# Sixteen-head attentions with their side work behind each quad of heads, and a spiking layer whose spikes TensorE counts

## The chip, the cores and the metric

The kernel runs on one core of a Trainium2 chip. The metric is the device time of one execution in microseconds (us). Engines are named as in the profile: PE (TensorE matmul), PEld (TensorE weight load), DVE (VectorE), ACT (ScalarE), POOL (GpSimd), SP (SyncE, which issues the DMAs here).

## The reference, cut to what matters

The whole is a stack of twelve small layers on 2048 tokens of 128 features, all in float32. Three of its stages matter here. The two sixteen-head attentions have heads of 8 features and 256 tokens a batch; the second is a mixture of two experts and stands twice in the stack, the first is causal and stands once:

```python
# L1 attention, 8 batches of 256 tokens, 16 heads of 8
scores = jnp.einsum('bhqd,bhkd->bhqk', q, k) * scale
scores = jnp.where(causal, scores, jnp.finfo(scores.dtype).min)
out = jnp.einsum('bhqk,bhkd->bhqd', jax.nn.softmax(scores, axis=-1), v)
return jnp.einsum('btc,cd->btd', out, w_out) + b_out
# L3 attention: the same without the mask, for M = 2 experts, mixed by mha_probs
scores = jnp.einsum('mbhtk,mbhsk->mbhts', q, kk) / jnp.sqrt(jnp.float32(KD))
ctx = jnp.einsum('mbhts,mbhsk->mbthk', jax.nn.softmax(scores, axis=-1), v)
# spiking layer (twice), y = relu(x W_fc)^2 W_proj, five steps
reset = spike_fn(mem - THRESHOLD)
mem_new = BETA * mem + y - reset * THRESHOLD
spk = spike_fn(mem_new - THRESHOLD)          # the output is the mean of spk over the steps
```

## The kernel before, in words

**Order.** Each engine runs a program written out by hand, stage after stage; a stage starts on an engine when all four compute engines have left the one before. Features lie on the partitions, tokens on the free axis. Within a stage the engines meet by semaphores; a wait stands in program order, so everything behind it on that engine waits too. All matmuls but some transposes go through the helper `mm`, so the trace gives them line 195. In the rows, x16 or x4 after a matmul counts instructions; one f32 matmul is two of them.

**SmallHeads** is the base class of `L1Attend` (8 units, one a batch) and `L3Attend` (16 units, two a batch, one an expert). A unit is 16 heads of one batch. `steps()` counts steps s; k = s // 16 is the unit and i = s % 16 the head of the score that is computed at this step. On TensorE a step holds, in this order: side work at certain i, the score of head i of unit k (two matmuls, bank 0, 1 or 5), at odd s the shifted scores of a pair of heads that lag 25 steps behind (`pair_at`, four matmuls into banks 2 to 4), and at every fourth step the weighing of four heads, called a quad here (`quad_at`: 16 f32 matmul instructions with 128x18 weights, which are the exponentials' partners, the values). Quads stand at i = 2, 6, 10, 14 in L3Attend and at i = 0, 4, 8, 12 in L1Attend.

What the other engines do with them: DVE takes the maxima of each score (L1229, or L1227 with the causal mask). A score of step s waits until the reduction of step s-3 is done. ACT takes the exponential of each head of a pair (L1208). A pair waits until the first exponential of the pair before is done (`exped`, 2g - 1). A quad waits for all exponentials of its four heads; in L1Attend it waits for POOL's causal selection of them (L1251).

The side work goes through PSUM bank 7, one group after the other, in both kernels:
- i=0: projection of q and k of unit k+2 (L1091); ACT adds the biases (L1182), POOL splits them into three bf16 parts (L1272 to L1279), and SP takes them through DRAM into the stacks (L1302, L1316), from which the scores of unit k+2 are computed.
- i=3: the maxima of unit k-1, which POOL split (L1258 to L1264), turned by a matmul with the identity (L1100); ACT copies them (L1190), SP moves them into the stacks (L1294). The first pair of the unit waits for that.
- i=5: the raw weighed sums of unit k-3, which ACT copied (L1214), transposed by four matmuls (L1110); DVE takes the reciprocals (L1235) and scales (L1238, raises `scaled`).
- i=7: the values of unit k (L1118), which wait for `scaled` of unit k-3; ACT copies them (L1373 in L1Attend, L1877 in L3Attend).
- i=9: the scaled context transposed again (L1124); ACT adds the bias (L1377, L1882).
- i=11, at the end of a batch: the output projection (`out_tensor`) and DVE's addition (`out_vector`, L1384, L1892).

**Spike.** After a norm, TensorE computes up and down projections of four chunks of 512 tokens, ACT relu and square and the copy of y (L970), and DVE five steps of the neuron a chunk: the membrane with opposite sign (L979), a comparison into the running count (L981), four times the decay (L983), the reset (L985) and the count (L987), then the addition to the residual (L989).

Of the kernel before, what the change touches and what calls it, by code (L numbers as in the profile page):

```python
# [926 lines left out]
class Spike(Stage):  # L927


    def __init__(self, k):  # L930
        super().__init__(k, "spike")
        a = self.arena
        self.h = a.take(TOKENS)
        self.norm = Norm(k, k.X, self.h, "eps5", a.take(TOKENS), a.take(TOKENS))
        self.relu = [a.take(4 * CHUNK) for _ in range(2)]
        self.y, self.mem, self.u, self.acc = (a.take(TOKENS) for _ in range(4))
        self.up, self.relued, self.squared = (self.sig(n, 4 * NCHUNK) for n in ("up", "relued", "squared"))
        self.down, self.copied = self.sig("down", NCHUNK), self.sig("copied", NCHUNK)

    def tensor(self, eng, ch):  # L940
# [4 lines left out]
        for c in range(NCHUNK):  # L945
            self.norm.wait_done(eng, max(c, 1))
            for j in range(4):
                self.wait_ge(eng, self.relued, 4 * c + j - 3)
                mm(ps[:, j, :], k.wp("L1f", "fcT")[:, j * P:(j + 1) * P], self.h[:, chunk(c)]).then_inc(self.up.sem, 1)
            ob = 4 + c % 2  # L950
# [5 lines left out]
            m.then_inc(self.down.sem, 1)  # L956

# [14 lines left out]
    def vector(self, eng, ch):  # L972
        k, V = self.k, self.k.nc.vector
        self.norm.vector(eng, ch)
        for c in range(NCHUNK):
            cs = chunk(c)
            y, mem, u, acc = self.y[:, cs], self.mem[:, cs], self.u[:, cs], self.acc[:, cs]
# [12 lines left out]


class SmallHeads(Stage):
# [9 lines left out]
    def __init__(self, k, name, group, tag, members, causal):  # L1002
# [23 lines left out]
        self.n1 = P if causal else SEQ  # L1026
        U, H = self.units, HEADS
# [16 lines left out]
    def steps(self):  # L1044

        for s in range(-2 * HEADS, HEADS * (self.units + 2) + 12):
# [29 lines left out]
    def heads_tensor(self, eng):  # L1076
        k_, ps, mm, T, U = self.k, self.k.ps, self.k.mm, self.k.nc.tensor, self.units
        for s, k, i in self.steps():
            if s == 1 - 2 * HEADS:
                self.route_tensor(eng)  # L1080
            u = k + 2
            if i == 0 and self.is_unit(u):
                self.wait_ge(eng, self.biased, u)
                self.wait_ge(eng, self.v_copied, k)
                self.wait_ge(eng, self.ctx_copied, k - 3)
                self.wait_out(eng, k - 4)
# [6 lines left out]
            u = k - 1  # L1093
            if i == 3 and self.is_unit(u):
                self.wait_ge(eng, self.mx_split, u + 1)
                self.wait_ge(eng, self.biased, min(k + 3, U))
                self.wait_ge(eng, self.ctx_copied, k - 3)
                self.wait_out(eng, k - 4)
# [3 lines left out]
            u = k - 3  # L1102
            if i == 5 and self.is_unit(u):
                self.wait_ge(eng, self.raw_copied, u + 1)
                self.wait_ge(eng, self.mx_copied, min(k, U))
                self.wait_ge(eng, self.v_copied, min(k, U))
                self.wait_out(eng, k - 4)
# [4 lines left out]
            if i == 7 and self.is_unit(k):  # L1112
                self.wait_ge(eng, self.biased, min(k + 3, U))
                self.wait_ge(eng, self.mx_copied, k)
                self.wait_ge(eng, self.scaled, k - 2)
                ms, b0 = self.member(k), k // self.members * SEQ
# [3 lines left out]
            if i == 9 and self.is_unit(u):  # L1120
                self.wait_ge(eng, self.scaled, u + 1)
                self.wait_ge(eng, self.v_copied, min(k + 1, U))
                for t in range(2):
                    o = T.transpose(ps[:, 7, t * P:(t + 1) * P], self.ctx[:, t * P:(t + 1) * P], k_.K("ident"))  # L1124
                o.then_inc(self.turned_again.sem, 1)
            if i == 11 and self.ends_batch(u):
                self.wait_ge(eng, self.ctx_copied, u + 1)
                self.out_tensor(u // self.members)
# [43 lines left out]
    def heads_scalar(self, eng):  # L1172
        k_, ps, S = self.k, self.k.ps, self.k.nc.scalar
        for s, k, i in self.steps():
            if s == 1 - 2 * HEADS:
                self.route_scalar(eng)
            u = k + 2
            if i == 0 and self.is_unit(u):
# [5 lines left out]
            u = k - 1  # L1184
            if i == 3 and self.is_unit(u):
# [5 lines left out]
            if i == 7 and self.is_unit(k):  # L1191
                self.wait_ge(eng, self.valued, k + 1)
                self.wait_ge(eng, self.weighed, self.QUADS * (k - 2))
                if k == 0:
                    self.wait_ge(eng, self.cleared, 1)
                    self.wait_prepared(eng)
                self.values_scalar(k).then_inc(self.v_copied.sem, 1)
            u = k - 3
            if i == 9 and self.is_unit(u):
# [16 lines left out]
    def heads_vector(self, eng, ch):  # L1216
        ps, V = self.k.ps, self.k.nc.vector
        for s, k, i in self.steps():
# [12 lines left out]
            u = k - 3  # L1231
            if i == 5 and self.is_unit(u):
# [7 lines left out]
            if i == 11 and self.ends_batch(u):  # L1240
                self.wait_ge(eng, self.summed, u // self.members + 1)
                self.out_vector(u // self.members)
# [103 lines left out]
class L1Attend(SmallHeads):  # L1346
# [28 lines left out]
    def context_scalar(self, eng, u):  # L1375
        self.wait_ge(eng, self.summed, u - 1)
        self.k.nc.scalar.activation(self.ctxT[u % 2], self.k.ps[:, 7, 0:SEQ], ACT.Identity, bias=self.k.C("vL1_0")).then_inc(self.ctx_copied.sem, 1)  # L1377

    def out_tensor(self, b):
        self.k.mm(self.k.ps[:, 7, 0:SEQ], self.k.wp("L1a", "wo"), self.ctxT[b % 2]).then_inc(self.summed.sem, 1)  # L1380
# [878 lines left out]
```

## Time and profile before

The time is the median of three runs. The profile comes from an execution of its own, in which some 1.7 us lie around the span.

| what | value |
|---|---|
| median of 3 runs (2144.8 to 2148.79) | 2145.94 us |
| profiled execution | 2153.13 us |
| its span | 2151.4 us |
| PE busy | 1720.4 us, 80% |
| DVE busy | 1294.6 us, 60% |
| ACT busy | 1156.7 us, 54% |
| POOL busy | 609.8 us, 28% |
| chain that ended last | PE 55%, DVE 17%, ACT 14%, issue 7% |

How to read it: a busy PE is not PE at its peak, since matmuls are pipelined and their ends are modelled; a matmul counts as busy until its last result is written. "Start to start" of two neighbours is therefore the better measure of what a group takes. An idle engine costs nothing unless it is on the chain that sets the end. The stages in question lie at about 999 to 1054 us and 1222 to 1279 us (Spike), 1054 to 1222 us (L1Attend), and, for the two L3Attend, their pairs run from about 1490 to 1710 us and from 1860 to 2083 us.

### The profile page before, as it was taken

Reading aid. Unit: us, or ns where it says so; the run is one execution under the profiler, and the core shown is the slowest. Engines: PE = TensorE matmul, PEld = TensorE weight load, DVE = VectorE, ACT = ScalarE, POOL = GpSimd, SP = SyncE. Lnnn points to the kernel's source line nnn. Section 1 sums busy time; section 2 is a strip of 40 time slices with the busy share of each in tenths; the row PEclk is TensorE's granted clock in tenths of the full one; section 3 lists DMA queues with packets and bytes.
Section 4 is the critical chain, followed back from the end, with each engine's and each line's share of the span. In section 5 each row is a group of like instructions: output and inputs, shape, how many; then the busy total and the mean of one; then the engine's idle time right before and its main releaser. Section 6 shows DMA issues by size and latency. Waiting matters only on the chain.

```text
span 2151.4 us, 36562 instructions
## 1 busy us (share of the span) xinstructions
PE 1720.4 (80%) x13656; PEld 904.2 (42%) x13656; DVE 1294.6 (60%) x2595; ACT 1156.7 (54%) x2714; POOL 609.8 (28%) x759
## 2 busy tenths in 40 slices
PE   5896889788898879879468864986999777799976
PEld 1554345533355425543234322333555352355435
DVE  4773477444676357734667276835878445577844
ACT  3664356434465436554336545562888726388862
POOL 2551055200453025410155202303332020333202
PEclk8998999999899899989768687995999978599997
DMA  4000000000000000000063000005444020544403
GB/s 170 16 17 6 0 16 16 12 0 1 16 12 16 1 11 16 12 6 0 8 117 65 2 0 1 0 0 100 95 95 88 2 78 0 109 96 93 80 2 98
DMA packets 55270, 79.19 MB, mean 37 GB/s; under 512 B 6004, under 2 KB 38996, under 8 KB 54584
## 3 DMA queue, kind: packets, MB, share of 16 engines
q1 hardware_dynamic: 52536, 68.47, 14.5%
q0 software_dynamic: 2560, 8.39, 1.4%
q8 instruction: 111, 1.82, 0.4%
q14 instruction: 63, 0.52, 0.1%
HBM read 50.59 MB, written 16.88 MB: 31 GB/s over the span
## 4 chain that ended last, share of the span: by engine, by line
PE 55%; DVE 17%; ACT 14%; issue 7%; POOL 3%; DMA 3%; SPq 0%; DVEq 0%; POOLq 0%; ACTq 0%
PE ps L195 51%; ACT arena L544 4%; ACT arena L1208 2%; DVE arena L1229 2%; PE ps L463 2%; DVE arena L600 2%; ACT arena L267 2%; ACT arena L269 2%; DVE arena L643 1%; DVE arena L985 1%; DVE arena L987 1%; ACT arena L263 1%; DVE arena L983 1%; DMA arena<-scratch 1%; DVE arena L612 1%
## 5 line engine op out<-in xcount | busy, mean ns | idle before, releaser
L195 PE MATMUL ps<-arena 32*64 32x128 f32 (+10 forms) x10192 | 724.0, 319 | 129.9 <-ACT arena L1208 28.1
L195 PEld LDWEIGHTS ps<-arena 128*18 128x18 f32 (+6 forms) x10192 | 412.3, 128 | 434.8 <-issue 120.7
L1229 DVE TENSOR_REDUCE arena<-ps 128x2 f32<-128x512 f32 x512 | 322.4, 684 | 111.1 <-PE ps L195 109.1
L195 PE MATMUL ps<-arena,w_L0f 128*128 128x512 f32 (+3 forms) x800 | 352.1, 573 | 39.5 <-ACT arena L291 14.5
L1208 ACT ACTIVATE arena<-ps 128x512 f32<-128x512 f32 (+1 forms) x640 | 333.8, 576 | 78.7 <-PE ps L195 69.5
L544 ACT ACTIVATE arena<-ps,arena 128x128 f32<-128x128 f32 x512 | 226.2, 461 | 137.8 <-DVE arena L645 137.8
L195 PEld LDWEIGHTS ps<-arena,w_L0f 128*128 128x128 f32 (+2 forms) x800 | 149.4, 204 | 174.4 <-issue 127.0
L195 PE MATMUL ps<-arena,const 128*128 128x512 f32 (+1 forms) x528 | 173.1, 618 | 60.7 <-DVE arena L1657 22.3
L715 POOL TENSOR_TENSOR arena<-arena 128x512 f32<-128x512 f32 x128 | 132.2, 1040 | 239.6 <-DVE arena L617 239.6
L600 DVE TENSOR_TENSOR arena<-ps,arena 128x1024 f32<-128x1024 f32 x128 | 153.3, 1206 | 21.1 <-PE ps L195 21.1
L555 ACT ACTIVATE arena<-ps 128x512 f32<-128x512 f32 x128 | 76.8, 600 | 126.1 <-DVE arena L600 123.4
L707 POOL TENSOR_TENSOR arena<-arena 128x512 f32<-128x512 f32 x64 | 81.2, 1269 | 218.3 <-DVE arena L600 215.5
L195 PEld LDWEIGHTS ps<-arena,const 128*128 128x128 f32 (+1 forms) x528 | 57.7, 156 | 161.9 <-issue 73.5
L643 DVE TENSOR_REDUCE arena<-ps 128x8 f32<-128x1024 f32 x64 | 78.3, 1223 | 71.8 <-PE ps L195 71.6
L612 DVE COPY arena<-ps 128x512 f32<-128x512 f32 x128 | 88.2, 689 | 48.4 <-PE ps L463 48.4
L463 PE MATMUL ps<-const,arena 128*128 128x128 f32 x512 | 80.2, 280 | 34.8 <-issue 26.5
L544 ACT ACTIVATION_READ_ACCUMULATOR arena<-ps,arena 128x1 f32 x512 | 106.5, 208 | 0.0
L1227 DVE CUSTOM_DVE_ANT_0 arena<-ps,masks_b 128x128 bf16<-128x128 f32 (+1 forms) x256 | 75.0, 353 | 43.6 <-PE ps L195 43.3
L463 PEld LDWEIGHTS ps<-const,arena 128*128 128x128 f32 x512 | 57.4, 142 | 96.3 <-issue 94.4
L195 PE MATMUL ps<-residual,const 128*128 128x512 f32 x96 | 58.4, 718 | 44.0 <-DVEq L2094 31.6
L1258 POOL CAST arena<-arena 128x32 bf16<-128x32 f32 x40 | 8.4, 209 | 286.1 <-DVE arena L1229 280.2
L708 POOL TENSOR_TENSOR arena<-arena 128x512 f32<-128x512 f32 x64 | 83.4, 1303 | 0.0
(223 smaller groups left out, 2150.0 us busy)
## 6 DMA issues: line engine op xcount, KB each, us to landing
scratch<-arena SPq DMA_DIRECT2D x40, 384.0 KB, 2.8
arena<-scratch SPq DMA_DIRECT2D x80, 192.0 KB
arena<-scratch SPq DMA_DIRECT2D x80, 128.0 KB
arena<-arena SPq DMA_DIRECT2D x64, 128.0 KB, 2.3
arena<-scratch SPq DMA_DIRECT2D x80, 88.0 KB
w_L0f<-in_L0f SPq DMA_DIRECT2D x2, 1557.0 KB, 12.3
arena<-arena SPq DMA_DIRECT2D x80, 12.0 KB
const<-in_const SPq DMA_DIRECT2D x1, 1276.0 KB, 7.6
```

Source lines behind the costliest of these rows:

```text
L195: return self.nc.tensor.matmul(o, lhsT, rhs, start=start, stop=stop, skip_group_check=True)
L463: o = k.nc.tensor.transpose(k.ps[:, 6, (2 * j + t) * P:(2 * j + t + 1) * P], self.prob[G % 2][:, 2 * p + j, t, :], k.K("ident"))
L544: o = S.activation(self.prob[G % 2][:, j, t, :], k.ps[:, j, t * P:(t + 1) * P], ACT.Exp, bias=self.negm[G % 2][:, at:at + 1], scale=rn[:, ...
L555: self.k.nc.scalar.activation(self.sq[i], self.k.ps[:, self.bank(G, 1 + second), :], ACT.Square).then_inc(self.squared.sem, 1)
L600: self.k.nc.vector.tensor_tensor(self.prod[n % 3].rearrange("p t (b s) -> p t b s", b=PER), x, tab, ALU.mult).then_inc(self.rotated.sem, 1)
L612: self.k.nc.vector.tensor_copy(self.probT[q % 4].rearrange("p j t s -> p (j t s)"), self.k.ps[:, 6, :]).then_inc(self.turn_copied.sem, 1)
L643: ch.did(V.tensor_reduce(self.mx[G % 2], ps[:, 0:4, 0:SEQ].rearrange("p j (t s) -> p j t s", t=2), AXX, ALU.max))
L707: G.tensor_tensor(y[:, i, :], first[:, 0, :], second[:, 1, :], ALU.add).then_inc(self.placed.sem, 1)
L708: G.tensor_tensor(y[:, i + 1, :], second[:, 0, :], first[:, 1, :], ALU.add).then_inc(self.placed.sem, 1)
L715: self.k.nc.gpsimd.tensor_tensor(pr, pr, rinv, ALU.mult).then_inc(self.scaled.sem, 1)
L1208: S.activation(self.pt[g % 4][:, e, 0:both], ps[:, self.shifted_bank(2 * g + e), 0:both], ACT.Exp, scale=self.scale).then_inc(self.exped.s ...
L1229: o = V.tensor_reduce(mx, ps[:, self.score_bank(s), :].rearrange("p (t s) -> p t s", t=2), AXX, ALU.max)
```

## The change

In SmallHeads the side groups keep their content and move. A new `other_at(s)` gives K, I = the unit and head of step s - `later`, with `later` = 2 in the causal stage and 0 in the other, and the groups are placed by them: projection of unit K+3 at I=15; output of unit K-4 at I=3, ahead of the turned maxima of unit K-1 at I=3; raw transposes of unit K-3 at I=7, with DVE's two instructions; values of unit K and context transposes of unit K-3 both at I=11. So each stands in the step after a quad. The second transposes and the output use the other half of bank 7. The waits that guard bank 7 are written anew; one new wait is ACT's value copy, which waits for the context transposes. In Spike the count is no longer kept by DVE: each comparison writes a bf16 tile, the reset is an addition of that tile, TensorE adds the five tiles by an identity matmul into PSUM bank 6 or 7 (`count`), and DVE adds this to the residual (`add`) one chunk later.

```diff
 class Spike(Stage)  # tensor
@@
+            if c >= 2:
+                self.count(eng, c - 2)
             ob = 4 + c % 2
...
+        self.count(eng, NCHUNK - 2)
+        self.count(eng, NCHUNK - 1)
+
+    def count(self, eng, c):
+        k = self.k
+        self.norm.wait_done(eng, 3)
+        self.wait_ge(eng, self.added, c - 1)
+        for i in range(SPIKE_STEPS):
+            self.wait_ge(eng, self.spiked, SPIKE_STEPS * c + i + 1)
+            k.mm(k.ps[:, 6 + c % 2, :], k.ident_b[:], self.fired[SPIKE_STEPS * (c % 2) + i], start=i == 0, stop=i == SPIKE_STEPS - 1).then_inc(self.counted.sem, 1)
@@ # vector
-            ch.did(V.tensor_scalar(mem, y, -1.0, None, ALU.mult))
-            ch.wait_ge()
-            V.tensor_scalar(acc, mem, -1.0, None, ALU.is_lt)
-            for _ in range(SPIKE_STEPS - 1):
-                ch.did(V.scalar_tensor_tensor(u, mem, BETA, y, ALU.mult, ALU.subtract))
+            self.wait_ge(eng, self.counted, SPIKE_STEPS * (c - 1))
+            V.tensor_scalar(fired[0], y, 1.0, None, ALU.is_gt).then_inc(self.spiked.sem, 1)
+            ch.did(V.scalar_tensor_tensor(u, y, -BETA, y, ALU.mult, ALU.subtract))
+            for i in range(1, SPIKE_STEPS):
                 ch.wait_ge()
-                ch.did(V.scalar_tensor_tensor(mem, mem, -1.0, u, ALU.is_lt, ALU.add))
+                self.wait_ge(eng, self.spiked, SPIKE_STEPS * c + i)
+                ch.did(V.tensor_tensor(mem, fired[i - 1], u, ALU.add))
                 ch.wait_ge()
-                ch.did(V.scalar_tensor_tensor(acc, mem, -1.0, acc, ALU.is_lt, ALU.add))
-            ch.wait_ge()
-            V.scalar_tensor_tensor(k.X[:, cs], acc, 0.5 / SPIKE_STEPS, k.X[:, cs], ALU.mult, ALU.add)
+                V.tensor_scalar(fired[i], mem, -1.0, None, ALU.is_lt).then_inc(self.spiked.sem, 1)
+                if i < SPIKE_STEPS - 1:
+                    ch.did(V.scalar_tensor_tensor(u, mem, BETA, y, ALU.mult, ALU.subtract))
+            if c:
+                self.add(eng, c - 1)
+        self.add(eng, NCHUNK - 1)
 class SmallHeads(Stage)
@@
+        self.later = 2 if causal else 0
@@
+    def other_at(self, s):
+        return (s - self.later) // HEADS, (s - self.later) % HEADS
@@ # heads_tensor
-            u = k + 2
-            if i == 0 and self.is_unit(u):
+            K, I = self.other_at(s)
+            u = K + 3
+            if I == 15 and self.is_unit(u):
...
-            u = k - 1
-            if i == 3 and self.is_unit(u):
+            u = K - 4
+            if I == 3 and self.ends_batch(u):
...
+                self.out_tensor(u // self.members)
+            u = K - 1
+            if I == 3 and self.is_unit(u):
...
-            if i == 5 and self.is_unit(u):
+            u = K - 3
+            if I == 7 and self.is_unit(u):
...
-            if i == 7 and self.is_unit(k):
+            if I == 11 and self.is_unit(K):
-                self.wait_ge(eng, self.scaled, k - 2)
+                self.wait_ge(eng, self.scaled, K - 2)
+                self.wait_out(eng, K - 4)
...
-            if i == 9 and self.is_unit(u):
+            if I == 11 and self.is_unit(u):
                 self.wait_ge(eng, self.scaled, u + 1)
-                self.wait_ge(eng, self.v_copied, min(k + 1, U))
+                self.wait_ge(eng, self.v_copied, min(K, U))
...
-            if i == 11 and self.ends_batch(u):
@@ # heads_scalar, values
+            if I == 11 and self.is_unit(K):
+                self.wait_ge(eng, self.valued, K + 1)
+                self.wait_ge(eng, self.turned_again, K - 2)
@@ # heads_vector
-            if i == 5 and self.is_unit(u):
+            if I == 7 and self.is_unit(u):
```

## Rows read from the trace of the kernel before

**Rows 1.** Windows: length, busy PE, PEld, DVE, ACT, POOL, PE clock, DMA share, GB/s.

```profile
1562.66:1589.78 27.12, 25.34 (x292) 13.77 (x293) 21.74 (x38) 22.08 (x45) 8.88 (x16) 1.00 0.48 92
```

**Rows 2.** Timeline, weight loads of the quads in L3Attend: start, length, what, idle before.

```profile
1573.43 0.56 PEld L195 LDWEIGHTS ps<-arena 128*18 128x18 f32 x16 [0.21 <-ACT arena L1208]
1576.24 0.56 PEld L195 LDWEIGHTS ps<-arena 128*18 128x18 f32 x16 [0.21 <-ACT arena L1208]
1579.59 0.57 PEld L195 LDWEIGHTS ps<-arena 128*18 128x18 f32 x16 [0.21 <-issue]
1582.60 0.56 PEld L195 LDWEIGHTS ps<-arena 128*18 128x18 f32 x16 [0.21 <-ACT arena L1208]
1586.47 0.56 PEld L195 LDWEIGHTS ps<-arena 128*18 128x18 f32 x16 [0.21 <-ACT arena L1208]
1590.32 0.56 PEld L195 LDWEIGHTS ps<-arena 128*18 128x18 f32 x16 [0.21 <-ACT arena L1208]
```

**Rows 3.** Timeline of PE, same stretch: the side groups.

```profile
1577.77 1.13 PE L195 MATMUL ps<-arena,w_L3m 128*128 128x256 f32 x4
...
1580.58 0.29 PE L195 MATMUL ps<-ident_b,arena 128*48 128x128 bf16 x2
1580.80 0.62 PE L195 MATMUL ps<-arena 48*128 48x256 bf16 x8
1581.38 0.63 PE L1110 MATMUL ps<-const,arena 128*128 128x128 f32 x4
...
1583.98 0.68 PE L195 MATMUL ps<-w_L3m,arena 128*128 128x128 f32 x4 [0.33 <-DVE arena L1238]
...
1585.34 0.41 PE L1124 MATMUL ps<-const,arena 128*128 128x128 f32 x2
...
1587.46 1.13 PE L195 MATMUL ps<-arena,w_L3m 128*128 128x256 f32 x4
```

**Rows 4.** Timeline of ACT, same stretch.

```profile
1575.05 2.22 ACT L1208 ACTIVATE arena<-ps 128x512 f32<-128x512 f32 x4
...
1578.94 0.84 ACT L1182 ACTIVATE arena<-ps,cols 128x256 f32<-128x256 f32 x2
...
1586.17 0.48 ACT L1882 ACTIVATE arena<-ps,arena 128x256 f32<-128x256 f32 x1
1586.53 1.10 ACT L1208 ACTIVATE arena<-ps 128x512 f32<-128x512 f32 x2
...
1589.13 2.22 ACT L1208 ACTIVATE arena<-ps 128x512 f32<-128x512 f32 x4 [0.94 <-PE ps L195]
```

**Rows 5.** Timeline of PE in L1Attend: the values of a unit.

```profile
1140.31 0.68 PE L195 MATMUL ps<-w_L1a,arena 128*128 128x128 f32 x4 [1.39 <-DVE arena L1238]
```

**Rows 6.** Timeline of POOL in L1Attend, and the quad of i=8 there.

```profile
1138.79 1.15 POOL L1279 TENSOR_TENSOR arena<-arena 128x512 bf16<-128x512 f32 x1
1139.89 1.81 POOL L1251 TENSOR_SCALAR_AFFINE_SELECT arena<-arena 128x512 f32<-128x512 f32 x3
...
1141.36 0.56 PEld L195 LDWEIGHTS ps<-arena 128*18 128x18 f32 x16 [0.16 <-issue]
```

**Rows 7.** Timeline of PE in the ramp of L1Attend: a projection.

```profile
1092.45 2.07 PE L195 MATMUL ps<-arena,w_L1a 128*128 128x256 f32 x4
```

**Rows 8.** Timeline of DVE in Spike, start of the last chunk.

```profile
1044.12 0.42 DVE L979 TENSOR_SCALAR arena<-arena 128x512 f32<-128x512 f32 x1
1044.57 0.43 DVE L981 TENSOR_SCALAR arena<-arena 128x512 f32<-128x512 f32 x1
1044.91 0.68 DVE L983 SCALAR_TENSOR_TENSOR arena<-arena 128x512 f32<-128x512 f32 x1
1045.63 0.69 DVE L985 SCALAR_TENSOR_TENSOR arena<-arena 128x512 f32<-128x512 f32 x1
1046.36 0.69 DVE L987 SCALAR_TENSOR_TENSOR arena<-arena 128x512 f32<-128x512 f32 x1
1046.97 0.68 DVE L983 SCALAR_TENSOR_TENSOR arena<-arena 128x512 f32<-128x512 f32 x1
```

More of the change, by code:

```diff
@@ L935, in __init__ @@
         self.relu = [a.take(4 * CHUNK) for _ in range(2)]
-        self.y, self.mem, self.u, self.acc = (a.take(TOKENS) for _ in range(4))
+        self.y, self.mem, self.u = (a.take(TOKENS) for _ in range(3))
+        self.fired = [a.take_bf16(CHUNK) for _ in range(2 * SPIKE_STEPS)]
         self.up, self.relued, self.squared = (self.sig(n, 4 * NCHUNK) for n in ("up", "relued", "squared"))
-        self.down, self.copied = self.sig("down", NCHUNK), self.sig("copied", NCHUNK)
+        self.down, self.copied, self.added = (self.sig(n, NCHUNK) for n in ("down", "copied", "added"))
+        self.spiked, self.counted = (self.sig(n, SPIKE_STEPS * NCHUNK) for n in ("spiked", "counted"))
     def tensor(self, eng, ch):
@@ L1044, in steps @@
     def steps(self):
-        for s in range(-2 * HEADS, HEADS * (self.units + 2) + 12):
+        for s in range(-2 * HEADS - 1, HEADS * (self.units + 3) + 6 + self.later):
             yield s, s // HEADS, s % HEADS
@@ L1174, in heads_scalar @@
         for s, k, i in self.steps():
-            if s == 1 - 2 * HEADS:
+            if s == 1 - 2 * HEADS + self.later:
                 self.route_scalar(eng)
-            u = k + 2
-            if i == 0 and self.is_unit(u):
+            K, I = self.other_at(s)
+            u = K + 3
+            if I == 15 and self.is_unit(u):
                 self.wait_ge(eng, self.projected, u + 1)
@@ L1183, in heads_scalar @@
                 o.then_inc(self.biased.sem, 1)
-            u = k - 1
-            if i == 3 and self.is_unit(u):
+            u = K - 1
+            if I == 3 and self.is_unit(u):
                 self.wait_ge(eng, self.mx_turned, u + 1)
@@ L1239, in heads_vector @@
                                 self.rinv.unsqueeze(3).to_broadcast([P, HEADS, 2, KD]), ALU.mult).then_inc(self.scaled.sem, 1)
-            if i == 11 and self.ends_batch(u):
+            u = K - 4
+            if I == 5 and self.ends_batch(u):
                 self.wait_ge(eng, self.summed, u // self.members + 1)
+                self.wait_ge(eng, self.mx_copied, min(K, self.units))
                 self.out_vector(u // self.members)
@@ L1376, in context_scalar @@
         self.wait_ge(eng, self.summed, u - 1)
-        self.k.nc.scalar.activation(self.ctxT[u % 2], self.k.ps[:, 7, 0:SEQ], ACT.Identity, bias=self.k.C("vL1_0")).then_inc(self.ctx_copied.sem, 1)
+        self.k.nc.scalar.activation(self.ctxT[u % 2], self.k.ps[:, 7, SEQ:2 * SEQ], ACT.Identity, bias=self.k.C("vL1_0")).then_inc(self.ctx_copied.sem, 1)
     def out_tensor(self, b):
-        self.k.mm(self.k.ps[:, 7, 0:SEQ], self.k.wp("L1a", "wo"), self.ctxT[b % 2]).then_inc(self.summed.sem, 1)
+        self.k.mm(self.k.ps[:, 7, SEQ:2 * SEQ], self.k.wp("L1a", "wo"), self.ctxT[b % 2]).then_inc(self.summed.sem, 1)
     def out_vector(self, b):
         X = self.k.X[:, b * SEQ:(b + 1) * SEQ]
-        self.k.nc.vector.scalar_tensor_tensor(X, self.k.ps[:, 7, 0:SEQ], self.k.C("L1_bo"), X, ALU.add, ALU.add).then_inc(self.added.sem, 1)
+        self.k.nc.vector.scalar_tensor_tensor(X, self.k.ps[:, 7, SEQ:2 * SEQ], self.k.C("L1_bo"), X, ALU.add, ALU.add).then_inc(self.added.sem, 1)
 class L2Ffn(Stage):
@@ L1881, in context_scalar @@
         self.wait_ge(eng, self.summed, u // M_EXPERTS)
-        self.k.nc.scalar.activation(self.ctxT[u % M_EXPERTS], self.k.ps[:, 7, 0:SEQ], ACT.Identity, bias=self.bvp[:, u:u + 1]).then_inc(self.ctx_copied.sem, 1)
+        self.k.nc.scalar.activation(self.ctxT[u % M_EXPERTS], self.k.ps[:, 7, SEQ:2 * SEQ], ACT.Identity, bias=self.bvp[:, u:u + 1]).then_inc(self.ctx_copied.sem, 1)
     def out_tensor(self, b):
@@ L1886, in out_tensor @@
         for j in range(M_EXPERTS):
-            m = k.mm(k.ps[:, 7, 0:SEQ], k.wp("L3m", "wo")[:, j * P:(j + 1) * P], self.ctxT[j], start=j == 0, stop=j == M_EXPERTS - 1)
+            m = k.mm(k.ps[:, 7, SEQ:2 * SEQ], k.wp("L3m", "wo")[:, j * P:(j + 1) * P], self.ctxT[j], start=j == 0, stop=j == M_EXPERTS - 1)
         m.then_inc(self.summed.sem, 1)
```

59 lines of the change are left out of this document (32 added, 27 removed).

## The prediction

> **What bounds the kernel now.** Three stages are touched: Spike (twice), L1Attend (once, 8 units of 16 heads) and L3Attend (twice, 16 units each). I read the page first (PE busy 80% of the span), then the windows of a steady stretch of L3Attend, where one batch (two units) takes 27.12 us with PE busy 25.34, ACT 22.08, DVE 21.74 [rows 1]. Read alone, that says "TensorE is the bound". The timelines say otherwise. The weighings of four heads (quads) are the x16 loads of 128x18 weights; their starts cut each unit into four cycles [rows 2]. Name them by what TensorE does in them today:
> - D without output: 1573.43 to 1576.24 = 2.81 us. No projection, transpose or value stands in it.
> - A (projection in the middle): 1576.24 to 1579.59 = 3.35.
> - B (turned maxima behind the quad, transposes of the raw sums in the middle): 3.01.
> - C (values behind the quad, transposes of the context in the middle): 3.87.
> - D with output behind the quad: 1586.47 to 1590.32 = 3.85.
>
> A quad whose row names ACT L1208 as releaser had to wait [rows 2]; only the one behind the projection (1579.59) did not, there TensorE itself was late. So the other cycles are ended by a loop, not by TensorE's throughput: quad, then one score and one pair of shifted scores, then ACT's two exponentials of that pair, then the next quad, which waits for them. What stands between a quad and the pair behind it lengthens the loop; what stands later, while ACT works on that pair, is covered.
>
> What each group takes of TensorE, start to next start, is its busy time less 0.07 (0.29 busy for the maxima, 1580.58 to 1580.80 = 0.22) [rows 3]: projection 1.06, maxima 0.22, transposes of the raw sums 0.56, values 0.61, transposes of the context 0.34, output 1.06. Test the reading on the five cycles, with 2.81 as the base. Behind the quad: output 1.06, cycle +1.04; maxima 0.22, cycle +0.20 (the 0.56 in the middle of B cost nothing); values 0.61, and they start 1.38 after their quad where output starts 0.99 after its own, so 0.39 of wait (for DVE L1238), cycle +1.06 (the 0.34 in the middle of C cost nothing). In the middle: projection 1.06 cost 0.54. So about 1.4 us of side work per unit is hidden today, and it is exactly what the change moves behind the quads.
>
> **L3Attend, part by part.** `later` is 0, quads stand at i = 2, 6, 10, 14, the groups move to i = 15, 3, 7, 11.
> - Projection, i=0 to i=15 (behind quad 14): TensorE's part makes the cycle 3.85 like the output's. ACT's two bias copies L1182 now stand ahead of the exponentials of the pair behind the quad, instead of behind them. They start 0.11 after the projection's slot (1577.77 + 1.06, then 1578.94) and take 0.84 busy less 0.12, 0.72, to the next exponential (on ACT the next start comes 0.12 before the end: L1882, 0.48 busy, 0.36 to the next) [rows 3, 4]: 0.99 + 1.06 + 0.11 + 0.72 = 2.88 after the quad. Behind the output the exponentials started 2.66 after the quad (1586.47 to 1589.13), so 0.22 shows. Cycle A 4.07, +0.72.
> - Maxima: stay at i=3. B stays 3.01.
> - Raw transposes, i=5 to i=7; DVE's L1235 and L1238 with them. 0.53 now shows; values leave this cycle and with them 1.06. C becomes 3.34, -0.53. The stall on DVE L1238 is really gone, nothing is late in its place: scaled is raised four heads before it is asked for.
> - Values and context transposes both at i=11: 0.61 + 0.34 = 0.95 behind quad 10. Besides, ACT's value copy L1877 now waits for the context transposes (turned_again), then L1882 follows, and the exponentials stand behind both on ACT: 0.99 + 0.95 + 0.11, L1877 0.4 to the next start (an estimate from L1882), L1882 0.36, so 2.81 after the quad, against 1.62 in D today (1573.43 to 1575.05) [rows 2, 4]. +1.19, cycle D 4.00.
> - Output: i=11 to i=3, 1.06 behind a quad before and after. 0. DVE's add (L1892) moves along, still off the loop.
>
> A full unit: +0.72 + 0 - 0.53 + 1.19 = +1.38 on 13.04. Not every unit has all of it: pairs run from step 25 to 279. 12 projections fall in there (+8.6); 15 raw transposes at 0.53 less 13 values at 1.06 and one at 0.6 (-6.4); 13 full value-and-context groups at 1.19, one with values and one with context alone, 1.0 together, and 0.7 at the tail, where the last context copy stands behind L1214 (+17.2). Sum +19.4 a stage, +38.8 for two. DVE (21.7 of 27.1) and the score banks have slack for it; the stacks of the next units are ordered by projections one step earlier, so the DMAs are not later.
>
> Bounds: below, the TensorE columns alone with no delay by ACT: 12 x 0.5 - 6.4 + 13 x 0.95 + 1.0 = +13 a stage, +26. Above, ACT's copies in full everywhere: 12 x 0.9 - 5.5 + 13 x 1.3 + 1.7 = +24 a stage, +48. I take 38.8, as the waits of ACT are written out in the code.
>
> **L1Attend.** Quads at i = 0, 4, 8, 12; with `later` = 2 the groups fall at i = 1, 5, 9, 13. The visible stall today is values on DVE L1238, 1.39 us [rows 5]. It goes, but the quad of i=8 needs POOL's selection of pair 3, and POOL works through the split of the maxima and of the projection in order before it (L1279 at 1138.79, then three selections 0.6 apart, the second one over near 1141.1 [rows 6]); the quad stands at 1141.36 now. As the projection copies are not earlier than today, this quad gains 0.3 at most. Against that, values and context transposes (0.95) and ACT's copies (0.3) come behind one quad, output and maxima behind another. +1.0 in the four units that still project, +0.3 in four others: +5.2. In the ramp the projection of unit 2 used to run while TensorE waited for the first stacks; at `later` = 2 it stands behind the first score. There such a projection takes 2.07, twice the 1.06 of later [rows 7], and the turned maxima come two heads later (they gate the first pair through SP's queue and a DMA): +2.5. Sum +7.7, bounds 0 (everything refills the 1.39 only) and +13 (the maxima's DMA also late for pair 9, 0.5 to 0.7 a unit).
>
> **Spike.** Per chunk today [rows 8]: 0.45 + 0.34, three rounds of 0.72 + 0.73 + 0.61, one of 0.72 + 0.73 + 0.72, and the addition, some 0.61 = 9.75; four chunks are 39.0, and DVE never waits after the first. After: compare 0.34 (next instruction doesn't wait), u 0.72, three rounds of sum 0.73, compare 0.34, u 0.72, then 0.73 + 0.34: 7.50, and an addition from PSUM, 0.67. The gain is in the compares: one source, 0.43 busy (like L979 and L981), where the forms with two sources take 0.69. Four chunks and three additions: 32.0; behind the last compare TensorE counts once (some 0.8, beside the third addition) and DVE adds once more, 0.8: 32.9. Saving 6.1 a stage, 12.2 for two. TensorE's counting (5 matmuls of 512 columns bf16, about 1.1 a chunk) stands in its queue ahead of the down projection and waits for DVE's fifth compare. For chunk 2 I get that compare at 1022.5, TensorE there at 1024.1; for chunk 3 1030.0 against 1032; y then arrives 0.7 us before DVE asks. Covered, but barely; uncovered it would cost 1 to 2 a stage. No row shows a bf16 output of a compare or a sum of bf16 and f32: between 0.43 and 0.69 for the first, 0.35 and 0.72 for the second. I take 0.43 and 0.69, the same forms in f32. By the ends: -1 to -11 a stage.
>
> **Sum.** 38.8 + 7.7 - 12.2 = +34.3. On the profiled execution (2153.13; span 2151.4 and 1.7 around it) that is 2187; it lies 7.2 above the median of 2145.94, so on the median 2180.
>
> **Rivals.**
> 1. TensorE is the bound after all, and moving is a gain. Each group costs about 0.1 beside its columns at each edge with the row-tiled scores (0.56 for four transposes, 0.34 for two: 0.12 is left over [rows 3]). Edges fall from 8 to 4 a unit (-0.5), the waits of values (0.4) and of the context transposes (0.2) go: -1.1 a unit, 28 units -31, L1 -8, Spike -12: 2095. For it: 25.34 of 27.12. Against it: in a bound TensorE the hidden 0.56 and 0.34 would show. The Trainium skill, TensorEngine Tiling (Array Packing), section Key Properties, says that changing the tiling mode drains TensorE; this is the rule that speaks for the move, and the 0.12 agrees with it, but by the rule alone the four edges would give 13 us in 28 units; it says nothing of a loop through ACT. 8 in 100.
> 2. The moved groups cost nothing where they land (ACT still busy with the pair before), only Spike shows: 2134. Against it: output, +1.04 for 1.06. 6 in 100.
> 3. The loop holds, but ACT's copies fit beside it and POOL doesn't bind in L1: 26 + 1 - 12.2 = +15, 2161. 18 in 100.
> 4. Forecast, with DVE's mixed forms at the slow end: +10 more, 2190. 8 in 100.
>
> **How the numbers follow.** The forecast holds 57 in 100, with its own range 2168 to 2192; gains and losses cancelling within 0.2% (4 us, what a measurement can tell) 2. Slower: 57 + 18 + 8 + 1 (the high bounds) = 84; faster 8 + 6 = 14. The range 2152 to 2194 leaves out rivals 1 and 2 and a little above.
>
> **What would show it.** L3: no value stall on DVE L1238, and yet quad-to-quad cycles of about 4.1, 3.0, 3.3 and 4.0, ACT waiting for PE longer ahead of L1208, units 14.4 instead of 13.04. If the cycles without the output are under 3.4 each, the loop reading is wrong and rival 1 or 2 holds. L1: units near 14 with the 1.39 stall gone and a quad waiting on POOL L1251. Spike: 33 us from the first to the last DVE instruction behind the norm, compares near 0.43, no wait of DVE for ACT's copy of chunks 2 and 3.

## The result, and the profile after

The changed kernel is slower: 2185.82 us median of 4 runs (2182.26 to 2190.27), against 2147.36 us, median of 4 (2144.8 to 2156.2), for the kernel before. The ratio is 1.0173 (95%: 1.0137 to 1.0209). Forecast were 2180 us, which is a ratio of 1.016; the direction and the size hold, and so does the main place, L3Attend. L1Attend's part came out near its forecast for other reasons than those given, as shown further down. The profiled execution took 2182.26 us, its span is 2180.5: 29.1 more than before in both, while the medians differ by 38.5. The experiments size that again, and say what hides between the two figures.

By stages, from the start of one stage's first table load on ACT (a load of function tables; L3Attend holds a second one within) to the next one's, ends read to 0.1 us:

| stage | before | after | difference | forecast |
|---|---|---|---|---|
| Spike, first | 54.8 | 48.4 | -6.4 | -6.1 |
| L1Attend | 168.6 | 171.6 | +3.0 | +7.7 |
| Spike, second | 58.0 | 51.6 | -6.4 | -6.1 |
| L3Attend, first | 278.9 | 297.3 | +18.4 | +19.4 |
| L3Attend, second | 280.3 | 299.9 | +19.6 | +19.4 |
| all others | | | +0.9 | 0 |

The first view to read again is the timeline of weight loads in L3Attend, the x16 loads of 128x18 of the quads; it answers to [rows 2]:

```profile
1576.51 0.57 PEld L195 LDWEIGHTS ps<-arena 128*18 128x18 f32 x16 [0.21 <-ACT arena L1246]
1580.59 0.57 PEld L195 LDWEIGHTS ps<-arena 128*18 128x18 f32 x16 [0.21 <-ACT arena L1246]
1583.60 0.57 PEld L195 LDWEIGHTS ps<-arena 128*18 128x18 f32 x16 [0.21 <-ACT arena L1246]
1587.05 0.57 PEld L195 LDWEIGHTS ps<-arena 128*18 128x18 f32 x16 [0.21 <-ACT arena L1246]
1590.98 0.56 PEld L195 LDWEIGHTS ps<-arena 128*18 128x18 f32 x16 [0.21 <-ACT arena L1246]
1595.06 0.56 PEld L195 LDWEIGHTS ps<-arena 128*18 128x18 f32 x16 [0.21 <-ACT arena L1246]
1599.13 0.56 PEld L195 LDWEIGHTS ps<-arena 128*18 128x18 f32 x16 [0.21 <-ACT arena L1246]
```

From 1576.51 the cycles are A 4.08, B 3.01, C 3.45, D 3.93, then A 4.08 and B with the output 4.07. The one quad that used to be late on TensorE's own account (`<-issue` in [rows 2]) is gone: now every quad waits for the exponentials, L1246. TensorE has not become the bound, it has been pushed further away from it. The timeline of PE and ACT in cycle D and in the next A shows what stands in the way (it answers to [rows 3, 4]):

```profile
1587.05 0.57 PEld L195 LDWEIGHTS ps<-arena 128*18 128x18 f32 x16 [0.21 <-ACT arena L1246]
...
1588.04 0.71 PE L195 MATMUL ps<-w_L3m,arena 128*128 128x128 f32 x4
...
1588.59 0.38 PE L1163 MATMUL ps<-const,arena 128*128 128x128 f32 x2
1589.06 0.49 ACT L1918 ACTIVATE arena<-ps,probs 128x256 f32<-128x256 f32 x1 [0.28 <-PE ps L1163]
1589.44 0.46 ACT L1923 ACTIVATE arena<-ps,arena 128x256 f32<-128x256 f32 x1
1589.79 2.23 ACT L1246 ACTIVATE arena<-ps 128x512 f32<-128x512 f32 x4
...
1590.98 0.56 PEld L195 LDWEIGHTS ps<-arena 128*18 128x18 f32 x16 [0.21 <-ACT arena L1246]
...
1593.14 0.84 ACT L1219 ACTIVATE arena<-ps,cols 128x256 f32<-128x256 f32 x2 [1.12 <-PE ps L195]
1593.87 2.22 ACT L1246 ACTIVATE arena<-ps 128x512 f32<-128x512 f32 x4
```

Behind the quad come values and context transposes, then both copies on ACT, and only then the exponentials for which TensorE stands still: they begin 2.74 after the quad (1587.05 to 1589.79; 2.81 was forecast, 1.62 was measured in this cycle before). Values no longer wait for DVE, and it buys nothing. In cycle A they begin 2.89 after the quad (2.88 forecast). The window of two units, one with output, as in [rows 1]:

```profile
1574.30:1604.34 30.04, 25.41 (x294) 14.00 (x292) 21.65 (x38) 22.25 (x45) 8.79 (x16) 1.00 0.40 85
```

The work is the same as before (PE 25.41 against 25.34, ACT 22.25 against 22.08, DVE 21.65 against 21.74), at the same granted clock, 1.00. The stretch is 2.92 longer, for 2.76 (twice 1.38) forecast.

In L1Attend (timeline) the 1.39 of [rows 5] is gone from the values, and the quad of the next rows waits for POOL's selection:

```profile
1144.42 0.84 PE L195 MATMUL ps<-arena 128*18 128x256 f32 x16 [0.96 <-POOL arena L1292]
...
1148.09 0.71 PE L195 MATMUL ps<-w_L1a,arena 128*128 128x128 f32 x4
...
1158.57 0.84 PE L195 MATMUL ps<-arena 128*18 128x256 f32 x16 [0.97 <-POOL arena L1292]
```

Spike, timeline of DVE, last chunk from its first comparison (against [rows 8]):

```profile
1040.36 0.42 DVE L996 TENSOR_SCALAR arena<-arena 128x512 bf16<-128x512 f32 x1
1040.69 0.68 DVE L997 SCALAR_TENSOR_TENSOR arena<-arena 128x512 f32<-128x512 f32 x1
1041.41 0.69 DVE L1001 TENSOR_TENSOR arena<-arena 128x512 f32<-128x512 bf16 x1
1042.14 0.43 DVE L1003 TENSOR_SCALAR arena<-arena 128x512 bf16<-128x512 f32 x1
```

The bf16 comparisons (L996, L1003) and the sum of bf16 and f32 (L1001) take the 0.43 and 0.69 that the forecast took.

### The profile page after: what moved, and what is told of

Its sections match the earlier page's. It is cut to its first block, busy times and chain, and to the rows that moved or that the text cites. A ratio compares the mean times of both kernels' runs of the same rounds, so it can differ in the third digit from the quotient of the medians.

```text
span 2180.5 us, 36753 instructions
## 1 busy us (share of the span) xinstructions
PE 1732.1 (79%) x13696; PEld 916.2 (42%) x13696; DVE 1281.1 (59%) x2587; ACT 1160.6 (53%) x2714; POOL 608.5 (28%) x759
## 4 chain that ended last, share of the span: by engine, by line
PE 55%; ACT 16%; DVE 13%; issue 8%; POOL 3%; DMA 3%; SPq 0%; DVEq 0%; POOLq 0%; ACTq 0%
PE ps L195 51%; ACT arena L1246 4%; ACT arena L544 4%; PE ps L463 2%; DVE arena L600 2%; ACT arena L267 2%; ACT arena L269 2%; DVE arena L643 1%; PE ps L1148 1%; DVE arena L1001 1%; DMA arena<-scratch 1%; ACT arena L263 1%; DVE arena L612 1%; PE ps L529 1%; DVE arena L1005 1%
## 5 line engine op out<-in xcount | busy, mean ns | idle before, releaser
L195 PEld LDWEIGHTS ps<-arena 128*18 128x18 f32 (+6 forms) x10192 | 419.9, 129 | 493.0 <-ACT arena L1246 140.6
L1246 ACT ACTIVATE arena<-ps 128x512 f32<-128x512 f32 (+1 forms) x640 | 333.8, 575 | 96.0 <-PE ps L195 80.9
L1265 DVE CUSTOM_DVE_ANT_0 arena<-ps,masks_b 128x128 bf16<-128x128 f32 (+1 forms) x256 | 74.2, 353 | 51.3 <-PE ps L195 51.1
L1219 ACT ACTIVATE arena<-ps,cols 128x256 f32<-128x256 f32 x80 | 33.6, 471 | 86.8 <-PE ps L195 86.8
```

The lines of the kernel that those rows point to most:

```text
L195: return self.nc.tensor.matmul(o, lhsT, rhs, start=start, stop=stop, skip_group_check=True)
L1246: S.activation(self.pt[g % 4][:, e, 0:both], ps[:, self.shifted_bank(2 * g + e), 0:both], ACT.Exp, scale=self.scale).then_inc(self.exped.s ...
```

## Experiments

A ratio is to the kernel before, timed on the same chip beside each kernel; the interval is 95%.

### The two parts apart, and the whole again

Spike alone: the kernel before with the new Spike class. Heads alone: the changed kernel with the old one.

> Kernel before with the new Spike class alone; attentions untouched. My forecast gave the counting by TensorE -6.1 us a stage, -12.2 for two; the markers of the changed kernel read -6.4 each, so -12.8: ratio 0.994. If those two figures were bought with something later (DMAs or weights that come late once Spike ends earlier), the ratio is nearer 1.000. If the mixed bf16/f32 forms ran at their slow end alone, -2 to -4 us, 0.999.

Measured: 0.993 (0.9907 to 0.9954), 2143.76 us against 2160.46. The Spike stages take 48.3 and 52.4, so 6.5 and 5.6 less than before. -12 us stand in the stages; the ratio says -15, and its interval (-10 to -20) holds both. The expectation, 0.994, holds.

> Changed kernel with the old Spike class; the attentions' new order alone. Loop theory (quad, score pair, exponentials, next quad): L3Attend +18.4 and +19.6 as in the changed kernel's profile, L1Attend +3, so +41 us, ratio 1.019. Rival (TensorE is the bound and the saved changes between row-tiled scores and whole-array products pay, the loss lies in Spike or elsewhere): at or under 1.000. If the two parts are independent, this and the Spike run add up to the changed kernel's ratio.

Measured: 1.0228 (1.0206 to 1.0250). The L3Attend stages are 299.2 and 299.3 long, +20.3 and +19.0. The expected 1.019 lies outside the interval: by the ratio the new order costs some 49 us, not 41. L1Attend takes 182.0 in this profile, 13.4 more than before, where +3 had been put; of that stage more below. The product of the two ratios, 0.993 x 1.0228 = 1.0156, is a little under the whole, by less than the intervals:

> The changed kernel once more beside the others, to size the whole effect on one chip. The two profiled executions differ by 29.1 us, the medians of the timed runs by 38.5. If the profile is right: ratio 1.0136; if the medians are: 1.018.

Measured: 1.0176 (1.0153 to 1.0200), 2196.6 against 2160.46. So the medians are right and the pair of profiles is not: 0.0176 x 2147 = 38 us. The likely reason why the profiles show 29 is that the time of one kernel goes with its granted clock. The kernel before took 2168.85 us in the run with mean clock 0.893 and 2150.35 in the one with 0.904, the changed kernel 2186.95 at 0.908 and 2196.37 to 2203.12 at 0.899 to 0.901. The profile before was taken at 0.898, the one after at 0.905. The kernel before took 2152.9 to 2160.91 at 0.899 to 0.901 on that chip, so at one clock the two are some 40 apart. The place where the clock shows most is L1Attend. The windows of that stage in five kernels follow (start and end, length, busy times, and the granted clock, which is the third number from the end). The kernel before:

```profile
1054.00:1222.60 168.60, 124.92 (x1184) 61.31 (x1184) 87.07 (x541) 83.54 (x190) 77.58 (x134) 0.74 0.32 61
```

Spike alone, the old order too:

```profile
1045.20:1204.90 159.70, 117.54 (x1184) 59.57 (x1184) 86.89 (x541) 83.18 (x190) 77.58 (x134) 0.80 0.33 64
```

The old order again, in the kernel "the order that follows" below:

```profile
1045.20:1210.50 165.30, 123.76 (x1185) 61.25 (x1185) 87.02 (x541) 83.67 (x190) 77.67 (x134) 0.75 0.32 62
```

The new order, in the changed kernel:

```profile
1049.40:1221.00 171.60, 124.61 (x1184) 64.53 (x1184) 86.31 (x541) 83.90 (x189) 77.67 (x134) 0.77 0.31 60
```

And in heads alone:

```profile
1052.50:1234.50 182.00, 138.07 (x1184) 70.23 (x1184) 86.40 (x541) 83.93 (x189) 77.83 (x134) 0.69 0.29 56
```

With the same instructions in the stage, but another Spike ahead of it, it takes 159.7 at 0.80 and 168.6 at 0.74: stretches at the lower of the two levels (0.50 of full speed, 1.2 GHz) are longer in one execution than in another. The +3.0 of the stage table compares a long specimen of the old order with a short one of the new.

### Is it the loop, or TensorE's throughput?

The same extra work of TensorE, four transposes whose results nobody reads, once behind a quad and once in the middle of the same cycle; the quads stand at i=6, 10 and so on.

```
+            if not self.causal and i == 11 and self.is_unit(k) and self.is_unit(k - 3) and not self.ends_batch(k - 3):
+                self.wait_ge(eng, self.ctx_copied, k - 2)
+                for t in range(4):
+                    T.transpose(ps[:, 7, t * P:(t + 1) * P], self.ctx[:, 0:P], k_.K("ident"))
             if self.is_unit(k):                 # the other kernel has i == 13 in the first line
```

> Kernel before, L3Attend alone: in the units that end no batch, four more transposes of 128x128 f32 whose results nobody reads, issued at i=11, right behind the quad of i=10. They take 0.56 us of TensorE. Loop theory: the cycle from this quad to the next, 2.81 in these units, becomes 3.3 to 3.4, and the unit 13.6 instead of 13.04. If TensorE's throughput bounds: the same +0.56. The pair of this run with the next one tells them apart.

> The same four extra transposes in the same cycle, at i=13, behind the score and the shifted pair that follow the quad of i=10. Loop theory: 0 to +0.1, the cycle stays at 2.8 to 2.9 and the unit at 13.0 to 13.1. TensorE's throughput as the bound: +0.56 here too, 3.4 and 13.6.

Timelines of weight loads and of PE, the four transposes (L1132) between their two quads, behind the quad:

```profile
1573.56 0.56 PEld L195 LDWEIGHTS ps<-arena 128*18 128x18 f32 x16 [0.21 <-ACT arena L1212]
1576.93 0.56 PEld L195 LDWEIGHTS ps<-arena 128*18 128x18 f32 x16 [0.21 <-ACT arena L1212]
...
1574.55 0.66 PE L1132 MATMUL ps<-const,arena 128*128 128x128 f32 x4
```

and in the middle:

```profile
1570.73 0.56 PEld L195 LDWEIGHTS ps<-arena 128*18 128x18 f32 x16 [0.21 <-ACT arena L1212]
1573.54 0.56 PEld L195 LDWEIGHTS ps<-arena 128*18 128x18 f32 x16 [0.21 <-ACT arena L1212]
...
1572.27 0.66 PE L1132 MATMUL ps<-const,arena 128*128 128x128 f32 x4
```

3.37 us from quad to quad against 2.81, which is the cycle without them. They don't wait in either place: behind the quad they start 0.99 after it, as the output does in [rows 2, 3]. The same four instructions cost their whole 0.56 in the one place and nothing in the other; all other cycles of the steady units are the same to 0.01. The stages are 281.9 and 285.1 long against 276.7 and 280.0. Of these 5.2 and 5.1 us, 3.9 are the seven cycles a stage that hold the transposes; the rest lies ahead of the steady units and behind them. Each kernel ran once, in 2174.09 and 2159.80 us, so there is no ratio, and the reading rests on the cycles. TensorE's throughput (rival 1) is not the bound here, and a group behind the quad isn't free (rival 2).

### ACT's place in the loop

The changed kernel; on ACT alone `u = K + 3, I == 15` becomes `u = K + 2, I == 0` for the bias copies, and I == 11 becomes I == 12 for the copies of values and contexts, so that each stands behind the exponentials of the pair.

> The changed kernel; on ScalarE alone the bias copies of the projection and the copies of values and contexts are issued one head later, behind the exponentials of the pair. TensorE's order is untouched. My terms: these copies ahead of the exponentials are 0.22 of cycle A (4.08 measured, to 3.86) and 0.24 of cycle D (3.93, to 3.7): 12 x 0.22 + 13 x 0.24 a stage, 11 to 12 us in the two L3Attend stages, ratio to the kernel before 1.0176 - 0.005 = 1.012. If ScalarE's place in the queue is worth nothing: 1.0176 and the same cycles.

Weight loads of the quads (timeline):

```profile
1575.90 0.56 PEld L195 LDWEIGHTS ps<-arena 128*18 128x18 f32 x16 [0.21 <-ACT arena L1246]
1579.75 0.57 PEld L195 LDWEIGHTS ps<-arena 128*18 128x18 f32 x16 [0.21 <-ACT arena L1246]
1582.76 0.57 PEld L195 LDWEIGHTS ps<-arena 128*18 128x18 f32 x16 [0.21 <-ACT arena L1246]
1586.21 0.56 PEld L195 LDWEIGHTS ps<-arena 128*18 128x18 f32 x16 [0.21 <-ACT arena L1246]
1589.86 0.56 PEld L195 LDWEIGHTS ps<-arena 128*18 128x18 f32 x16 [0.21 <-ACT arena L1246]
```

A is 3.85 (4.08 before this edit), D 3.65 (3.93): 0.23 and 0.28, for 0.22 and 0.24 expected. The L3Attend stages are 293.6 and 295.9 long, 3.7 and 4.0 less, not the 5.5 to 6 of the sum over all units. From the first quad to the last they are 5.1 and 6.0 shorter, as expected; the rest is given back ahead of the first quad (0.6 and 0.9 later) and behind the last (0.9 and 1.2 more). The ratio is 1.0155 (1.0127 to 1.0183). It misses the 1.012 expected, just outside the interval, and can't be told from the changed kernel's; the cycles can.

### All side work into the middle

The loop says which order would be good: no group behind a quad. The changed kernel with its groups at projection I=0, maxima and contexts I=4, raw transposes I=8, output and values I=12, DVE's addition I=15 (`later` = -2 in L1Attend, so that they stand alike to its quads).

> Changed kernel, but each group of side work of the attentions is issued in the middle of a cycle, two heads away from the quad: projection at i=0, maxima and context transposes at i=4, raw transposes at i=8, output and values at i=12. Loop theory: 0.56 of a group hides there, all of the maxima and of the raw and context transposes, a part of projection, values and output; cycles of about 3.35, 2.85, 2.85, 2.9 us in L3Attend, a unit 12.0 to 12.4 without output where before had 13.04 and the changed kernel 14.47: 30 to 40 us under before with Spike's 12.8 in it, ratio 0.981 to 0.986. Rival (TensorE's throughput bounds, edges between kinds of work cost): as many edges as before, so only Spike's 12.8 shows, ratio 0.994; that one also keeps the unit at 13.0.

Measured: 0.9984 (0.9959 to 1.0010), not 0.981 to 0.986. The expectation fails. The quads in its timeline, and two rows of PE:

```profile
1562.25 0.56 PEld L195 LDWEIGHTS ps<-arena 128*18 128x18 f32 x16 [0.21 <-issue]
1566.05 0.56 PEld L195 LDWEIGHTS ps<-arena 128*18 128x18 f32 x16 [0.21 <-issue]
1570.53 0.57 PEld L195 LDWEIGHTS ps<-arena 128*18 128x18 f32 x16 [0.21 <-issue]
1573.41 0.56 PEld L195 LDWEIGHTS ps<-arena 128*18 128x18 f32 x16 [0.21 <-ACT arena L1249]
1577.04 0.56 PEld L195 LDWEIGHTS ps<-arena 128*18 128x18 f32 x16 [0.21 <-issue]
1579.97 0.56 PEld L195 LDWEIGHTS ps<-arena 128*18 128x18 f32 x16 [0.21 <-ACT arena L1249]
...
1568.74 1.10 PE L195 MATMUL ps<-arena,w_L3m 128*128 128x256 f32 x4 [1.09 <-DVE stream L1936]
...
1576.50 1.60 PE L195 MATMUL ps<-arena 51*128 51x256 bf16 x22 [0.57 <-DMA arena<-arena]
```

The cycles with contexts and maxima (2.88) and with values (2.93) are as short as expected. Two others are not. After an output, the projection waits 1.09 for DVE's addition, which I had put one head ahead of it (cycle 4.48 for 3.35). And the maxima, one head later than before, reach the first pair of the unit late by their DMA: 3.63 for 2.85. Two placings of mine, no limit of TensorE. So the L3Attend stages are 278.9 and 282.1 long, no shorter than before. Spike's 12 us are in this kernel too (0.993 alone), yet the whole is at 0.9984: L1Attend takes 172.1 at a clock of 0.71, and the waits found in L3Attend don't say why.

### The order that follows

The new Spike with the old order, but in L3Attend: values from i=7 to 8; output (of unit k-4) and contexts together at i=12 instead of 11 and 9, in the two halves of bank 7; the addition at 13. Projection 0, maxima 3 and raw transposes 5 stay.

```
-            if i == 7 and self.is_unit(k):
+            if i == self.values_at and self.is_unit(k):       # 7 in L1Attend, 8 in L3Attend
...
+            if not self.causal and i == 12 and self.ends_batch(b):   # b = k - 4
+                self.out_tensor(b // self.members)
-            if i == 9 and self.is_unit(u):
+            if i == self.ctx_at and self.is_unit(u):          # 9, 12
```

> The new Spike with the attentions of the kernel before, but in L3Attend the values at i=8 instead of 7 and output and context transposes together at i=12 instead of 11 and 9 (output one unit later), all in the middle of a cycle; the maxima stay at i=3, one head earlier than in the all-in-the-middle kernel, whose unit lost 0.85 us at the first pair to their DMA and 1.1 in batch ends to a DVE addition. Loop theory: cycles A 3.35, B 3.01, C 2.93, D 2.85, and 3.7 with output: units 12.1 and 13.0 instead of 13.04 and 14.08, 0.9 to 1.0 us times 14 units, -25 us in two stages, with Spike -38 to -40: ratio 0.982. TensorE's throughput as the bound: the columns are the same, only Spike shows, 0.993.

```profile
1542.01 0.56 PEld L195 LDWEIGHTS ps<-arena 128*18 128x18 f32 x16 [0.21 <-ACT arena L1244]
1545.37 0.56 PEld L195 LDWEIGHTS ps<-arena 128*18 128x18 f32 x16 [0.21 <-issue]
1548.38 0.56 PEld L195 LDWEIGHTS ps<-arena 128*18 128x18 f32 x16 [0.21 <-ACT arena L1244]
1551.31 0.56 PEld L195 LDWEIGHTS ps<-arena 128*18 128x18 f32 x16 [0.21 <-ACT arena L1244]
1554.88 0.56 PEld L195 LDWEIGHTS ps<-arena 128*18 128x18 f32 x16 [0.21 <-issue]
```

Measured: 0.9836 (0.9813 to 0.9858), 2121.34 us. The 0.982 of the loop lies in the interval, the 0.993 of a bound TensorE doesn't. The timeline gives A 3.36, B 3.01, C 2.93, D 3.57 with output and 2.81 without: four of them to 0.04 of the expectation, the output 0.13 better. The L3Attend stages take 267.1 and 266.3, some 12.5 less than with the old order.

### L1Attend's order alone, and a better one

L1Attend of the changed kernel in the kernel just shown:

> The best kernel so far (new Spike, L3Attend with values at i=8 and output with contexts at i=12), but L1Attend as in the changed kernel. It prices L1Attend's new order alone. My forecast gave +7.7 (bounds 0 and +13). The profiles so far: old order 159.7 us at a granted clock of 0.80, 165.3 to 165.7 at 0.75 to 0.76, 168.6 at 0.74; new order 171.6 and 171.7 at 0.77 and 0.75, 182.0 and 182.2 at 0.69 and 0.72. If order and clock both count: +6 at one clock and some +12 on the mean, as the new order also has more of its stretches at half clock: the ratio goes from 0.9836 to 0.988 to 0.989. If the difference in L1Attend is chance in the clock: 0.984 to 0.986.

Measured: 0.9872 (0.9839 to 0.9906), stage 171.5 us at clock 0.75. Against 0.9836 that is +0.0036, 7.8 us; the two intervals overlap, so the timing alone doesn't separate them. Nor does it choose between the two expectations, 0.988 to 0.989 and 0.984 to 0.986: the interval holds both. The stages say more: at a clock of 0.75 the old order took 165.3 and the new one 171.5, +6.2.

But the mean clock of the stage hides where the time goes. The quads cut the stage into four parts: up to the first quad, 16 cycles in which the last four projections fall, 15 cycles more, and the tail (timelines of weight loads; the granted clock from the windows between the same quads):

| kernel | order | to the first quad | 16 cycles (clock) | 15 cycles (clock) | tail |
|---|---|---|---|---|---|
| before | old | 55.0 | 53.3 (0.90) | 53.0 (0.75) | 7.3 |
| Spike alone | old | 54.7 | 50.7 (0.96) | 48.4 (0.86) | 5.9 |
| the order that follows | old | 54.9 | 51.3 (0.93) | 51.7 (0.77) | 7.3 |
| changed | new | 54.5 | 63.4 (0.83) | 46.5 (0.85) | 7.2 |
| changed, again | new | 53.6 | 64.3 (0.77) | 46.5 (0.86) | 7.2 |
| heads alone | new | 54.6 | 70.3 (0.67) | 47.5 (0.82) | 9.6 |
| this one | new | 54.0 | 67.8 (0.71) | 41.8 (1.00) | 7.9 |

The new order loses 10 to 20 us in the 16 cycles and wins back up to 11 in the 15. The windows of single units at full clock: with a projection, in the old order (the order that follows) and in the new one (the changed kernel), then without one, in the old order (the same kernel) and in the new one (this kernel):

```profile
1120.10:1133.11 13.01, 10.92 (x149) 6.13 (x146) 10.49 (x68) 9.20 (x23) 9.28 (x17) 1.00 0.51 99
1144.42:1158.57 14.15, 10.95 (x146) 6.47 (x146) 10.33 (x68) 9.32 (x22) 9.32 (x17) 1.00 0.47 90
1151.45:1164.37 12.92, 9.76 (x144) 5.38 (x143) 10.42 (x68) 8.62 (x21) 5.91 (x13) 1.00 0.17 25
1168.69:1180.95 12.26, 9.97 (x143) 5.75 (x143) 10.32 (x70) 8.59 (x20) 5.91 (x13) 1.00 0.05 10
```

That is +1.14 and -0.66 a unit. Four of each make +2; the rest of the loss goes with the clock. The four profiles of the new order have 0.67 to 0.83 in the 16 cycles, the five of the old one 0.90 to 0.96 (the two kernels with extra transposes have 0.93), so the clock there goes with the order and not only with the execution. Why it does isn't shown.

Last, the same moves for L1Attend, whose quads stand at i = 0, 4, 8, 12: `(7, 9, 11, 3) if causal` becomes `(10, 14, 15, 4) if causal` for values, contexts and output, addition, and the units by which the output is behind.

> The best kernel so far, with L1Attend's side work moved as in L3Attend: values from i=7 to 10, contexts from 9 to 14, output from 11 to 14 one unit later, the addition at 15; quads stand at i = 0, 4, 8, 12, so 10 and 14 are the middle of a cycle. TensorE's wait of 1.4 us a unit for DVE L1274 should go, and nothing new comes behind a quad: up to 1.4 x 8 = 11 us off L1Attend, ratio 0.979. If POOL's selections or ScalarE's exponentials end those cycles, it goes to them: 0 to -3 us, 0.982 to 0.984.

Measured: 0.9801 (0.9769 to 0.9833; 0.979 expected), 2112.06 us against 2153.92 for the kernel before; the stage takes 160.6 us at clock 0.79, where the old order took 159.7 at 0.80 and 165.3 at 0.75. So part of it may be clock: the gain over 0.9836 (0.0035, some 7.5 us) is inside the intervals, and whether order or clock brought it stays open. TensorE's waits for DVE's scaling in the stage fall from 6.9 us (five of up to 1.4, not the eight expected) to 1.0. Against L1Attend's order of the changed kernel the case is clear: the kernels of the last two runs differ in this stage alone and were timed on the same chip, 2123.63 to 2131.62 us with that order and 2108.42 to 2113.71 with this one, 13.8 between the medians. This is the best kernel of the study, 42 us under the one before.

## Why the prediction was right

- **What bounds.** The loop quad, pair, exponentials, next quad was read from five cycle lengths of one trace. The pair of runs with extra transposes shows it for L3Attend: 0.56 behind the quad, 0.00 in the middle. Rival 1 also had its price twice: 0.12 is left over for a group, so for both of its edges, and it was counted at each edge.
- **L3Attend.** Forecast cycles 4.07, 3.01, 3.34, 4.00; measured 4.08, 3.01, 3.45, 3.93. C is 0.11 too low: 0.53 was taken for the raw transposes behind the quad, and they cost 0.64 over 2.81: the exponentials start 2.19 after the quad instead of 1.62, and the four of them are busy 2.30 instead of 2.22, for a reason that no run shows. D is 0.07 too high: the exponentials follow the quad after 2.74, not 2.81. The unit is 14.47 for 14.42, the stages +18.4 and +19.6 for +19.4.
- **ACT's copies.** 0.22 and 0.24 of the cycles; moving them gave 0.23 and 0.28. Rival 3 falls with that, and with the total.
- **L1Attend.** The profile shows +3.0 for +7.7; at the same mean clock it is +6.2, and by time +7.8 with an interval that is as wide. That this is near the forecast is luck. The steps came as put: the 1.39 for DVE gone, a quad waiting for POOL, and a unit that projects at 14.15 for "near 14", +1.14 for +1.0. But the units that don't project are 0.66 shorter, for +0.3; the first quad comes 54.5 us into the stage, 55.0 before, so the 2.5 set down for the ramp weren't paid there; and the time that takes the place of both goes with the lower clock in the 16 cycles, for which the sum had no term.
- **Spike.** -6.4 for -6.1. Compares with a bf16 output take 0.43 and the sum of bf16 and f32 0.69, the values taken (rival 4's slow compare is out). A chunk with its addition takes 8.07 (1032.29 to 1040.36), 8.17 was forecast. From the first comparison to the end of the last addition it is 32.6 us, for 32.9. DVE never waits for y.
- **The sum.** +34.3 forecast. The stages give +38.0 for L3Attend, -12.8 for Spike, +6 to +8 for L1Attend: 31 to 33. The medians say +36 to +38.5. L1Attend can hold most of the difference: its mean is 165.0 us in the five profiles of the old order (159.7 to 168.6) and 174.2 in the four of the new one (171.5 to 182.0), +9, which makes the sum 34. With such a spread that is a likely account, not a shown one.

## What to carry to other kernels

A busy share of 93% did not make TensorE the bound: in a loop over two in-order engines, find the instruction that the other engine waits for, and put side work behind it, while that engine is at work, not ahead of it. A stall that an order removes (0.39 here in L3Attend) is worth nothing if the order lengthens the loop; check each cycle's length, not the list of waits. And when groups are moved into the free place, go through their consumers too (an addition, a DMA): two such waits ate L3Attend's whole gain of the first try. An order can also go with another granted clock in a stage, so look at the clock part by part before calling a difference chance.

## What the runs showed of the hardware

- The time of one and the same kernel goes with the granted clock: 2150.35 us at a mean of 0.904, 2168.85 at 0.893. A stage with the same instructions, in five kernels, took 159.7 at 0.80 and 165.3 to 168.6 at 0.76 to 0.74. A single pair of profiles misjudged a difference of 38 us by 9.
- With the counting products on TensorE the granted clock in Spike is 0.94 in the first such stage and 0.89 to 0.90 in the second, in each of the five profiles looked at; without them it is 0.85 and 0.82, in all four. DVE's instructions stand back to back there, so the time follows them.
- An order of the same work can go with a lower clock: in L1Attend the 16 cycles with the last projections had 0.90 to 0.96 in five profiles of the old order and 0.67 to 0.83 in four of the new one.
- A comparison on DVE with one f32 source took 0.43 us for 128x512 with a bf16 as with an f32 result; the sum of a bf16 and an f32 source took 0.69, like two f32 sources.
